# Filler products on TensorE, a reordered routing, and the last residual added by TensorE in a one-core Perceiver block

## The reference, cut to what matters

```python
x = x + cross_attention(layernorm(x), ctx_768, ...)      # 32 batches, 257 context rows of 384
x = x + self_attention(layernorm(x), ...)                # 16 heads, RoPE, 32 tokens per batch
x = x + ffn(layernorm(x), gate_w, balance_bias, w1, w2)

def ffn(xf, gate_w, balance_bias, w1, w2):               # 8 experts, 512 -> 1024 -> 512
    scores = sigmoid(xf @ gate_w.T + balance_bias)
    top, idx = top_k(scores, 2)
    comb = zeros.at[token, idx].add(top / (top.sum(-1) + 1e-6))
    h = silu(einsum('td,ehd->teh', xf, w1))
    return einsum('te,ted->td', comb, einsum('teh,edh->ted', h, w2))
```

## Time and profile before

| | |
|---|---|
| Median of 3 runs | 537.12 us (536.85 to 538.25) |
| The profiled execution, its own time | 536.98 us |
| Its span in the trace | 534.4 us |
| PE busy | 490.4 us, 92% of the span |
| DVE busy | 374.6 us, 70% |
| ACT busy | 254.2 us, 48% |
| POOL busy | 111.3 us, 21% |
| Mean granted TensorE clock | 0.963 of full speed |

### The profile page before, as it was taken

The page is one execution under the profiler, slowest core; times in us unless marked ns, Lnnn a source line. Parts: engine busy times, 40 slices in busy tenths (PEclk is TensorE's granted clock), DMA queues, the critical chain, the costliest instruction groups (busy, mean ns, idle before and its releaser), DMA issues.

```text
span 534.4 us, 11347 instructions
## 1 busy us (share of the span) xinstructions
PE 490.4 (92%) x3746; PEld 286.0 (54%) x3747; DVE 374.6 (70%) x849; ACT 254.2 (48%) x396; POOL 111.3 (21%) x86
## 2 busy tenths in 40 slices
PE   5998889999999999976879899999999999999994
PEld 2753546555675776735565444445444454444443
DVE  5778898777859998888787886763746637673230
ACT  1313555643359293846732745544625446552230
POOL 1032212012160322200663022111121111121112
PEclk9898999999999999986869999999999999999997
DMA  8999697900009996256842589894885947843333
GB/s 309 405 397 380 242 389 262 371 3 1 1 1 381 379 383 219 72 212 229 288 189 100 154 270 260 270 257 129 230 243 141 258 112 218 238 82 73 59 59 40
DMA packets 55201, 110.95 MB, mean 208 GB/s; under 512 B 24416, under 2 KB 25600, under 8 KB 50048
## 3 DMA queue, kind: packets, MB, share of 16 engines
q1 hardware_dynamic: 25296, 87.80, 45.4%
q10 hardware_dynamic: 25568, 12.94, 10.1%
q0 software_dynamic: 4304, 9.77, 8.6%
HBM read 75.82 MB, written 29.43 MB: 197 GB/s over the span
## 4 chain that ended last, share of the span: by engine, by line
PE 52%; DVE 27%; issue 6%; DMA 5%; ACT 4%; POOL 3%; SPq 2%; DVEq 1%; ACTq 0%; POOLq 0%
PE bank L787 18%; PE bank L769 17%; DMA ctx_region<-in_ctx 4%; PE bank L372 3%; PE bank L540 3%; PE bank L556 3%; DVE wbuf L1614 2%; DVE small L1164 2%; POOL small L1757 2%; DVE small L1161 2%; DVE small L1131 1%; PE bank L751 1%; DVE ctx_region L1411 1%; PE bank L633 1%; DVE ctx_region L1413 1%
## 5 line engine op out<-in xcount | busy, mean ns | idle before, releaser
L769 PE MATMUL bank<-wbuf,ctx_region 128*128 x480 | 106.9, 379 | 0.0
L1614 DVE SCALAR_TENSOR_TENSOR wbuf<-ctx_region,wbuf 128x2048 f32 (+1 forms) x28 | 62.9, 2288 | 29.4 <-ACT wbuf L963 28.0
L1856 POOL DMA_INDIRECT out<-misc,ints x21 | 39.8, 1894 | 203.0 <-ACT misc L1046 144.4
L769 PEld LDWEIGHTS bank<-wbuf,ctx_region 128*128 128x128 f16 x480 | 46.1, 98 | 51.9
L963 ACT ACTIVATE wbuf<-ctx_region 128x2048 f32 (+1 forms) x28 | 52.0, 1902 | 27.6 <-issue 17.2
L1757 POOL TENSOR_TENSOR small<-small 128x2 f32<-128x2 f32 (+2 forms) x25 | 27.4, 1098 | 162.9 <-DVE small L1137 160.1
L1065 ACT ACTIVATE ctxT_region<-bank 128x512 f32<-128x512 f32 x42 | 25.0, 597 | 67.0 <-PE bank L769 56.0
L787 PE MATMUL bank<-wbuf,xn 128*128 x240 | 53.4, 379 | 0.9 <-DVE xn L1714 0.9
L787 PE MATMUL bank<-wbuf,actT 128*128 x240 | 53.4, 379 | 0.0
L787 PEld LDWEIGHTS bank<-wbuf,xn 128*128 128x128 f16 x240 | 23.5, 98 | 29.4 <-issue 1.7
L1708 DVE CAST ctxT_region<-ctxT_region 128x1024 f16<-128x1024 f32 x21 | 14.6, 694 | 34.9 <-ACT ctxT_region L1065 34.9
(11 more groups left out here) (232 smaller groups left out, 858.9 us busy)
## 6 DMA issues: line engine op xcount, KB each, us to landing
ctx_region<-in_experts SPq DMA_DIRECT2D x28, 1024.0 KB
routed_rows<-ctxT_region SPq DMA_DIRECT2D x1, 16900.0 KB, 50.8
ctxT_region<-in_ctxT SPq DMA_DIRECT2D x8, 1542.0 KB, 11.1
ctx_region<-in_ctx SPq DMA_DIRECT2D x8, 1536.0 KB, 8.9
ctx_region<-routed_rows ACTq DMA_DIRECT2D x21, 260.0 KB, 3.2
wbuf<-in_experts SPq DMA_DIRECT2D x4, 1024.0 KB
out<-x ACTq DMA_DIRECT2D x8, 256.0 KB
wbuf<-in_wqT SPq DMA_DIRECT2D x4, 256.0 KB, 5.3
```

Source lines behind the costliest of these rows:

```text
L769: mm = nc.tensor.matmul(bank[half][:, :], xgT[:, b, x_part, k * P:(k + 1) * P], w16[:, ds(at + (w_part + k * EH + half * 512), 512)], star ...
L1614: nc.vector.scalar_tensor_tensor(w16[:, ds(at + (LOW + n * PIECE), PIECE)], src_[:, piece], W_SCALE, w16[:, ds(at + (HIGH + n * PIECE), PI ...
L1856: nc.gpsimd.indirect_dma_start(out, bass.IndirectOffsetOnAxis(idx[:, slot_no:slot_no + 1].bitcast(U32), axis=0), y_out[:, slot_no, :], Non ...
```

## The change

`unread(b, count)` is new: `count` products of 128x128 by 128x512 in float16, of the identity by itself, into a PSUM bank that nobody reads. It stands at eight places on PE. In `attend` of pair 2 it stands behind the wait for `z`. Three stand in front of waits around `features_T` and `logits` of pair 2, one in front of `features_T` of pair 3, one in front of `choices_before(2)`, one in front of `first_tile_product`, one in `join_values`.

For the last pair PE adds the residual: `last_residual` multiplies `x` by 256 times the identity in float32 into banks 4 and 5, and the projection accumulates on it. DVE takes the statistics straight from PSUM; ACT copies `x` out (`last_out`), between its pieces of `cut_high`; DVE normalises out of PSUM, tile by tile, after `last_out` of that tile.

In the routing, the marks of tiles 0 to 3 are split in two; `choose_gates(1)` and `slots_out(1)` move behind `last_features_low(1)`; the first cut of DVE (`cut_low`, piece 0) moves behind `slots_out(2)`; two of `first_rows`'s tiles move from in front of `features_T(3)` to behind it; `first_tile_product` no longer waits for `rt_slots` and goes through k on the outside, halves on the inside; ACT's piece 2 moves behind the load of the silu table and piece 3 behind `first_rows_out(0)`; one scatter moves from ahead of POOL's last inverse root to behind it.

```diff
+            def unread(b, count):
+                pe.wait_ge(s["ident16_set"], 1)
+                for _ in range(count):
+                    nc.tensor.matmul(bank[b][:, :], ident16[:, :], ident16[:, None, :].to_broadcast([P, 4, P]), start=True, stop=True,
+                                     skip_group_check=True)
...
                         join_biases()
+                        unread(4, 6)
                         pe.wait_ge(s["sc_nb"], 2)
...
                 elif pair + 1 < PAIRS:
                     pe.wait_ge(s["z"], 2 * pair)
+                if pair + 2 == PAIRS:
+                    unread(0, 8)
                 for t in range(2):
                     pe.wait_ge(s["ao_hi"], 2 * pair + t + 1)
...
+            def last_residual():
+                pe.wait_ge(s["residual_step"], 1)
+                pe.wait_ge(s["x_plus_sbo"], TILES)
+                pe.wait_ge(s["x_post"], TILES - 2)
+                for t in range(2):
+                    tile = TILES - 2 + t
+                    nc.tensor.matmul(bank[4 + t][:, :], ident_scaled[:, :], x[:, tile * D:(tile + 1) * D], start=True, stop=False,
+                                     skip_group_check=True)
...
                     scores(pair)
+                    unread(2, 6)
                     features_T(pair - 1)
+                    last_residual()
+                    unread(2, 3)
                     logits(pair - 1)
+                    unread(2, 4)
...
-            first_rows(0, range(0, ROUTED[0][1]))
+            first_rows(0, range(0, 2))
+            unread(6, 5)
             features_T(PAIRS - 1)
+            first_rows(0, range(2, ROUTED[0][1]))
             pe.wait_ge(s["z"], TILES - 2)
+            pe.wait_ge(s["x_post"], TILES)
             logits(PAIRS - 1)
             first_rows(0, range(*ROUTED[1]))
+            unread(6, 8)
             choices_before(2)
...
-                pe.wait_ge(s["rt_slots"], len(ROUTED))
                 pe.wait_ge(s["xgT0"], 1)
...
+            unread(4, 4)
             first_tile_product()
...
+            def last_out(t):
+                tile = TILES - 2 + t
+                act.wait_ge(s["residual_step"], t + 2)
+                nc.scalar.activation(x[:, tile * D:(tile + 1) * D], bank[4 + t][:, :], ACT.Copy, scale=1.0 / W_SCALE)\
+                    .then_inc(s["x_post"], 1)
...
-            cut_high(expert0, 2 * EXPERT, (0, 1, 2), 0)
+            cut_high(expert0, 2 * EXPERT, (0,), 0)
+            last_out(0)
+            cut_high(expert0, 2 * EXPERT, (1,), 0)
+            last_out(1)
             features_out(PAIRS - 1)
             features_high(PAIRS - 1)
             gate_exp(2)
-            cut_high(expert0, 2 * EXPERT, (3,), 0)
             nc.scalar.activation(sc_nb, neg_half[:, 0:2], ACT.Silu)
+            cut_high(expert0, 2 * EXPERT, (2,), 0)
...
+            def very_last_stats():
+                for t in range(2):
+                    dve.wait_ge(s["sy_ps"], TILES - 1 + t)
+                    nc.vector.bn_stats(stats[:, t, :], bank[4 + t][:, :]).then_inc(s["residual_step"], 1)
+                    if t == 0:
+                        mark_at(0)
+                        mark(range(0, 2))
+                dve.wait_ge(s["residual_step"], 3)
+                norm_mean(stats, mv, ve, s["ln4_ve"], 2, EPS * W_SCALE * W_SCALE)
+                mark(range(2, ROUTED[0][1]))
+            def very_last_scale():
+                dve.wait_ge(s["ln4_rstd"], PAIRS)
+                dve.wait_ge(s["xf_lo"], 2 * (PAIRS - 1))
+                for t in range(2):
+                    dve.wait_ge(s["x_post"], TILES - 1 + t)
+                    normalise(ln4_n[:, t, :], bank[4 + t][:, :], mv[:, t, 0:1], rstd[:, t:t + 1]).then_inc(s["xf"], 1)
...
             choose_scores(1)
-            choose_gates(1)
             logits_out(PAIRS - 1)
             choose_rank(2)
-            slots_out(1)
             last_features_low(0)
             place(2)
-            mark(2)
+            mark_at(2)
+            mark(range(*ROUTED[2]))
             last_features_low(1)
-            cut_low(expert0, 2 * EXPERT, (0,), 0)
+            choose_gates(1)
+            slots_out(1)
             choose_experts(2)
             choose_scores(2)
             choose_gates(2)
             slots_out(2)
+            cut_low(expert0, 2 * EXPERT, (0,), 0)
...
-                    scatter(0, first_to_store[0:2])
+                    scatter(0, first_to_store[0:1])
                     features_low(pair - 1)
-                    scatter(0, first_to_store[2:3])
+                    scatter(0, first_to_store[1:2])
...
-            scatter(0, first_to_store[3:])
+            scatter(0, first_to_store[2:])
```

More of the change, by code:

```diff
@@ L633, in attend @@
                             nc.tensor.matmul(bank[4 + t][:, :], ao[:, 0, t, k, :], swo16[:, w_part, k, :],
-                                             start=(k == 0 and w_part == 0), stop=False)
+                                             start=(pair + 1 < PAIRS and k == 0 and w_part == 0), stop=False,
+                                             skip_group_check=True)
                     pe.wait_ge(s["ao_lo"], 2 * pair + t + 1)
@@ L637, in attend @@
                         mm = nc.tensor.matmul(bank[4 + t][:, :], ao[:, 1, t, k, :], swo16[:, 0, k, :],
-                                              start=False, stop=(k == KC - 1))
+                                              start=False, stop=(k == KC - 1), skip_group_check=True)
                     mm.then_inc(s["sy_ps"], 1)
@@ L708, in no_rows, with first_rows @@
                                      skip_group_check=True)
-            def first_rows(n, tiles):
+            def first_rows(n, tiles, parts=(0, 1)):
                 for tile in tiles:
                     pe.wait_ge(s["hot"], tile + 1)
-                    pe.wait_ge(s["xf_lo"], tile + 1)
-                    for part in range(2):
+                    for part in parts:
+                        pe.wait_ge((s["xf_hi"], s["xf_lo"])[part], tile + 1)
                         for k in range(KC):
@@ L720, in first_rows @@
                                                   start=False, stop=(tile == TILES - 1), skip_group_check=True)
-                if tile == TILES - 1:
+                if tile == TILES - 1 and 1 in parts:
                     mm.then_inc(s["xgT_ps"], 1)
@@ L734, in _ @@
             first_rows(1, range(0, 2))
-            first_rows(0, range(*ROUTED[2]))
+            for part in range(2):
+                first_rows(0, range(*ROUTED[2]), (part,))
             def first_tile_product():
                 at = 2 * EXPERT
-                pe.wait_ge(s["rt_slots"], len(ROUTED))
                 pe.wait_ge(s["xgT0"], 1)
                 for w_part, x_parts in ((HIGH, (0, 1)), (LOW, (0,))):
-                    for half in range(2):
-                        for k in range(KC):
-                            if w_part == LOW:
-                                pe.wait_ge(s["w1_lo"], k // 2 + 1)
-                            else:
-                                pe.wait_ge(s["w_hi"], k // 2 + 1)
+                    for k in range(KC):
+                        pe.wait_ge(s["w1_lo"] if w_part == LOW else s["w_hi"], k // 2 + 1)
+                        for half in range(2):
                             for x_part in x_parts:
@@ L753, in first_tile_product @@
                                                       stop=(k == KC - 1 and w_part == LOW), skip_group_check=True)
-                        if w_part == LOW:
-                            mm.then_inc(s["h_ps"], 1)
+                            if w_part == LOW and k == KC - 1:
+                                mm.then_inc(s["h_ps"], 1)
             def experts_of(tile):
@@ L1087, in _ @@
             first_rows_out(0, s["xgT0"], 1)
+            cut_high(expert0, 2 * EXPERT, (3,), 0)
             silu(0)
@@ L1469, in last_stats @@
                         choose_experts(0)
-                    if pair + 1 == PAIRS and t == 0:
-                        mark(0)
                 norm_mean(stats, mv, ve, s["ln4_ve"], 2)
@@ L1560, in place, with mark_at, mark @@
                 then(tt(slot[:, some], bank[within][:, lo * E:hi * E].rearrange("p (t e) -> p t e", e=E), base[:, some, :], ALU.add))
-            def mark(n):
-                lo, hi = ROUTED[n]
-                some = slice(lo, hi)
+            def mark_at(n):
+                some = slice(*ROUTED[n])
                 dve.wait_ge(s["rt_sel"], n + 1)
                 then(nc.vector.scalar_tensor_tensor(hot_at[:, some], sel[:, some, 0], -CHOSEN, slot[:, some, 0], ALU.mult, ALU.add))
-                for tile in range(lo, hi):
+            def mark(tiles):
+                for tile in tiles:
                     ts(hot[:, tile, :], late("places"), hot_at[:, tile:tile + 1], None, ALU.is_equal).then_inc(s["hot"], 1)
@@ L1665, in _ @@
                     choose_rank(0)
-                last_stats(pair)
-                if pair + 2 < PAIRS:
-                    join(pair + 1, 0)
-                last_scale(pair)
```

(19 more changed lines are left out.)

13 lines of the change are left out of this document (8 added, 5 removed).

## The result

The changed kernel takes 539.34 us (median of 20 executions; the kernel before, 20 beside them, 536.94): ratio 1.0039, 95% interval 1.0024 to 1.0055. It is slower by 0.4%, clear of noise though small; the forecast was 533.3, faster. The profiled execution took 538.29 us, with a span of 536.3 (before 536.98 and 534.4).

What follows compares the result with a forecast made beforehand. DVE was taken to set the pace until PE saturates at 311.21 us. `cut_hidden(0)` was to start 4.2 us earlier, less 0.4 for scatters: -3.8 from 536.98 gives 533.3 us, own range 532.3 to 534.6, wider range 531.5 to 536.0.

Steps and rivals of the forecast that it cites:

- Scatters, +0.4 of 4.2: Group 1's later slots and scatters, which ACT waits for: up to 0.8 us of the 4.2 gained lost, 0.4 taken.
- the scatters become the bound: Rival: a last landing near 293 takes all 4.2 us; with 2 us lost, 535.3 us; chance 0.08.
- T = 272.2: When DVE's next cut after the last pair's choices is due: 272.2 us for 274.54, 2.3 us gained.
- slower: Rival: fillers run at half clock on the path around 246 and 266 to 276 us; +2.6, 539.7 us; chance 0.07.
- Eight products behind z: Unread products in pair 2's `attend`, reached only when `z` is there: +1.7 us on the path.
- The clock around attend: Fillers around `features_T(2)` and `logits(2)` keep full clock for the second tile's `attend` and projection: -1.8 us, 0 if not.
- Statistics from PSUM: Last pair: L1464 and its wait behind the marks go, -1.7 us; reading PSUM costs +0.15, bounds 0 and 0.3.
- Logits at full clock: Last pair's logits take 1.85 us instead of 3.56: -1.7 us, ending at 266.9 instead of 269.7.
- Transposes of the last pair: Transposes of pair 3 end at 264.1 us, 1.6 us earlier than before.
- First tile product ready: `first_tile_product`, made in pieces while waiting for DVE's low parts, ends at 281.6 us for 286.74.
- PE saturated from 307: Sign of being right: PE busy without a stop from 307 us, where before it was from 311.
- all clock back: Rival: all 27.3 us of half-clock work lies on the path, worth 13.7 us; 523.5 us, chance 0.02.

Runs made afterwards that it cites:

- e18: Changed kernel with gates and slots of group 1 back ahead of the last features' low parts, on chip C: 532.73 us, ratio to before 0.9932.
- e14: The changed kernel again, unedited, on chip C: 535.86 us, ratio to before 0.9966.
- e19: Changed kernel without the eight unread products behind PE's wait for `z` in pair 2, on chip C: 534.89 us, ratio to before 0.9969.
- e3: Changed kernel without the eight unread products behind PE's wait for `z` in pair 2, on chip A: 538.25 us, ratio to before 1.0000.
- e5: Changed kernel with slots of group 1 back and without the eight products behind `z`, on chip B: 530.25 us, ratio to before 0.9891.
- e12: The program of e5 without any unread product, on chip A: 537.30 us, ratio to before 0.9988.
- e13: The program of e5 again, on chip A: 536.35 us, ratio to before 0.9963.
- e2: Kernel before with only the unread products added, at the same waits, on chip A: 539.91 us, ratio to before 1.0050.
- e1: Changed kernel with every unread product taken out, on chip A: 540.44 us, ratio to before 1.0046.
- e10: Changed kernel with the transfers of x to out for tiles 6 and 7 issued later, on chip A: 539.70 us, ratio to before 1.0041.
- e11: The program of e5 with the transfers of x to out for tiles 6 and 7 issued later, on chip A: 535.70 us, ratio to before 0.9960.
- e17: The program of e5 again, on chip C: 532.10 us, ratio to before 0.9895.
- e9: Changed kernel with the 16 products of `first_rows` back behind the last logits, on chip B: 536.65 us, ratio to before 0.9982.

## Why the prediction was wrong

Two steps failed. One is a term that was mis-sized, the other wasn't in the sum at all.

**Scatters, +0.4 of 4.2.** Shown: about 3, by e18 against e14 (the edit also takes 1.2 us of DVE's work out of the way, which in e14 nobody waited for). The forecast put the last scatter at 286 to 287 with a landing near 288, and compared that with ACT's copy at 292.29. In e14 the last ends at 287.98 and the transfer behind the wait starts at 289.76. Between it and the copy ACT issues two transfers and reads addresses: 1.8 us (289.76 to 291.57) that can't move ahead of the landing. Landing at 289.76 is thus not 2.5 us of slack but 0.7. The slots also came at 274.35, not 273.4, 1 us late with T; in e18, with nothing of the third group in front of them, at 270.0. The rival "the scatters become the bound" had the mechanism, a chance of 0.08 and 535.3 us; e14 measured 535.86. It should have been the likeliest case: its own limit, a landing at 293, left out the work between landing and copy. (Eight scatters with 0.3 us between them end 0.3 earlier than the rival's sums say, at 294.2 and 284.0; in e14 they took 12.85 us, from 275.13.)

**T = 272.2.** T is the moment at which DVE is done with the last pair's low parts. In the record it was 276.42, of which 3.9 us are the late signal. No row of before shows such a wait, and no rival had it. It takes the gain of the logits' clock (1.8 us) and 2 us more. On chip C, T was 273.22 with the logits ending at 268.18 instead of 266.9; from there on 5.0 us, forecast 5.3.

The sum, then: -3.8 forecast; scatters about 2.5 more, and it is -1.3 (e14: -1.4). The late signals add what A and C differ by, 3.4 to 4.3, and it is +2.0 to +2.9 (the record: +2.4). That it fits so well is in part luck: the 3 us of the scatters hold lost clock behind ACT's wait (below), and other terms missed by 0.2 to 0.7 us each. It is luck, too, that the rival "slower" named 539.7: in it the clock stayed at half at the logits and around `attend`, and the traces show both gains instead.

Of the signs that the forecast gave for being wrong, two came in the record's trace: stretches of 0.50 around 250 and 274 (not in e14's), and ACT waiting for the scatters past 288.5 (292.95, in e14 289.76). And there `choices_before(2)` is released by DVE, late with the logits, and not by PE.

**Term by term**, in the record's trace:
- Eight products behind z: forecast +1.7. L644 starts 2.2 us after z, part of them at half clock (from 232.8). At the end they cost 1.0 (e19) to 1.1 (e3; the comparison is with the record's 539.34), neither clear of the spread.
- The clock around attend: forecast -1.8. From z to the last projection's end 29.50 us against 29.56, with the 2.1 us of products in it: right, though the clock still fell once, at 249.9.
- Statistics from PSUM: forecast -1.7, and +0.15 for reading PSUM. Its own figures, 0.91 and 0.67, add up to 1.6. From the projection's end to the normalising 2.15 us instead of 3.65: -1.5. But the two normalising instructions take 1.53 us instead of 1.00, 0.26 more each, and both lie on the path: 0.53, beyond the upper bound of 0.3. The rule of the Trainium skill, VectorE: DVE Perf Modes, "Why PSUM operands drop a tier", points the right way: the trace agrees that this instruction is slower out of PSUM, by 0.26 us.
- Logits at full clock: forecast 1.85 us, measured 1.90.
- Transposes of the last pair: forecast to end at 264.1; they end at 265.29, in e14 at 265.54. The two normalising instructions are 0.4 us of that. In e14 0.9 more is `z`, which comes at 231.71 (before 230.84); executions differ there for reasons ahead of this stretch (230.75 in e5, 235.82 in e3).
- First tile product ready: forecast 281.6, in e14 282.63, T being 1.0 later; it stands in pieces and waits for DVE's L1672, as forecast.
- PE saturated from 307: no. ACT's and DVE's delay leaves PE idle 3.48 us before L373 at 304.88, the clock is at half around it (304.5 to 307.9), and L796 takes 5.82 us. In e14 it is the same with 6.8 us at half clock (300.9 to 307.7):

```profile
301.69 1.03 PE L373 MATMUL bank<-ident,ctxT_region 128*128 128x128 f16 x8 [3.48 <-DVE ctxT_region L1773]
302.94 1.03 PE L373 MATMUL bank<-ident,ctxT_region 128*128 128x128 f16 x8 [0.23 <-DVE ctxT_region L1775]
303.77 7.28 PE L796 MATMUL bank<-wbuf,ctx_region 128*128 x24
```

In e18 the idle time is 1.60 us, the clock stays full, and the 24 products take 5.34. This loss was not in the sum; against 5.34 it costs 0.5 us in the record and 1.9 in e14.

```profile
297.89 0.62 PE L373 MATMUL bank<-ident,ctxT_region 128*128 128x128 f16 x8 [1.60 <-DVE ctxT_region L1773]
...
299.61 5.34 PE L796 MATMUL bank<-wbuf,ctx_region 128*128 x24
305.84 5.35 PE L814 MATMUL bank<-wbuf,xn 128*128 x24 [0.89 <-DVE xn L1779]
```

The rival "all clock back" was wrong as a time: the mean clock rose by 0.018, the time didn't follow. The unread products are worth 0.95 us on chip A (e12, e13) where they don't stand on the path.

**What stays open.** Why PE's semaphores rise late on chip A. Shown: it goes with the chip. For the last logits it is so in 7 of the 7 executions profiled there with the new routing and residual, and in 0 of 8 on B and C; A was used twice, with B between. The late signal of the logits also needs something of the new kernel, since e2 on A has none there; but e2 has one of 1.3 us at the first rows. The kernel before was not profiled on A; all that is known is that its time there is that on B and C within 0.6 us. It is not the unread products (e1 and e12 have the late logits), and not the transfers of x (e10, e11). Whether it takes the new routing, the new residual or both wasn't tried on A, nor were the rows behind the logits, nor a kernel with its scatters elsewhere. On which chip the 20 executions of the record ran isn't known; its trace shows the late signal.

The best kernel is that of e5, e13 and e17, the change with the slots of group 1 back and nothing behind `z`: 1.1% faster than before on B and C, 0.4% on A.

## What to carry to other kernels

Following one event through a reordered stretch is not enough: for each engine that meets the path again later, take the arrival it waits for plus everything that it must still issue behind that wait, and compare that with where it would stand. The slots came 4.3 us later behind other work of DVE (e14, e18), the last of eight transfers 4.4 us later, and it was worth 3 us of the kernel. Unread products can help in a wait that they fill; behind a wait they delay the work by their full length there (2.2 us) and cost some part of it at the end. And a result that only one chip gave is not yet a property of the kernel: the same program was 1.1% faster than its predecessor on two chips and 0.4% on a third.

## What the runs showed of the hardware

- On one chip a semaphore of PE rose 3.9 to 4.0 us after the end that the profile gives to the product which raises it (its last rise; the one before it, for the first tile, 4.7 to 4.8), in all seven profiled executions with the new routing and residual, and in none of eight on two others. Of six of the seven both rises are in the trace, one for each tile: they lie 0.09 us apart, the products' ends 0.89. Meanwhile PE's next instructions start about 0.7 us or twice that apart (e13: 269.20, 269.93, 270.64, 272.06). Elsewhere in the kernel the same chip shows such delays of 1.0 to 3.3 us, the other two none over 0.25 us.
- Normalising 128x512 float32 out of PSUM takes 0.77 us, out of SBUF 0.50; statistics 0.70 out of PSUM, 0.69 out of SBUF.
- Mean clock and time go together within one kernel: over the 64 executions of the kernel before that stand beside e1 to e9 (0.954 to 0.972) a fitted line falls 2.5 us for 0.01. Between kernels it doesn't hold: the unread products brought 0.010 and 0.95 us (e12, e13), and the changed kernel 0.018 and no gain.
